# Vision tower on one core: attention weights turned three heads at a time and placed by nine transfers instead of six

## What is computed

```
h = patches @ W.T + b, class token in front, + pos_embed          # 64 x 37 x 256
q, k, v = h @ Wq, h @ Wkv                                         # 16 heads of 64
sim = q k^T * scale;  sim = sim + cope(q, sim, pos_emb)           # cope: gates, sum from the right, table lookups
attn = softmax(sim);  out = attn v;  h = layernorm(h + out @ Wout + b_out)
router = softmax(h @ router_w), top 2 of 8 experts, shared and routed feed-forward, layernorm
```

## Time and profile before

| | |
|---|---|
| median of 3 runs | 717.65 us (717.54 to 722.87) |
| the profiled execution's own time | 716.74 us |
| its span, first to last instruction | 715.0 us |
| TensorE busy, matmuls | 683.1 us, 96% of the span |
| VectorE busy | 489.1 us, 68% |
| ScalarE busy | 422.9 us, 59% |
| mean granted TensorE clock | 0.994 of full speed |

### The profile page before, as it was taken

How to read it: one execution, slowest core, us unless ns; L and a number is a source line. 1 busy time by engine, 2 the same in 40 slices (tenths; PEclk the granted TensorE clock), 3 DMA queues, 4 the chain that set the end, 5 groups by cost and what they waited for, 6 DMA issues and landing times.

```text
span 715.0 us, 14167 instructions
## 1 busy us (share of the span) xinstructions
PE 683.1 (96%) x4762; PEld 587.2 (82%) x4763; DVE 489.1 (68%) x1027; ACT 422.9 (59%) x730; POOL 123.0 (17%) x156
## 2 busy tenths in 40 slices
PE   8998999999999999999999999889999999999995
PEld 5897697978879696987969697658898999998884
DVE  3376787878978787897878789788962222332657
ACT  1563767576586657667675656544217777774453
POOL 2100000000000000000000000010014777775130
PEclk9999999999999999999999999999999999999998
DMA  9720321514132141414112103227304555552811
GB/s 274 224 66 16 77 60 35 95 47 103 49 80 74 36 94 48 99 54 94 43 41 58 47 18 104 85 88 237 128 15 108 146 138 131 145 130 57 286 69 54
DMA packets 81958, 67.16 MB, mean 94 GB/s; under 512 B 50646, under 2 KB 73196, under 8 KB 81928
## 3 DMA queue, kind: packets, MB, share of 16 engines
q1 hardware_dynamic: 76906, 56.30, 29.3%
q0 software_dynamic: 4224, 9.71, 4.5%
q10 hardware_dynamic: 798, 0.76, 0.3%
HBM read 35.60 MB, written 15.75 MB: 72 GB/s over the span
## 4 chain that ended last, share of the span: by engine, by line
PE 44%; DVE 34%; issue 9%; ACT 7%; DMA 4%; DVEq 1%; ACTq 0%; SPq 0%; POOLq 0%
PE ps_S L1419 11%; DVE table L1925 7%; PE ps_S L1150 7%; PE ps_S L1431 5%; PE ps_S L1352 3%; DVE u L1908 3%; DVE bit L1917 3%; PE ps_S L930 3%; PE ps_X L1025 2%; DVE nb L1937 2%; DVE nb L1940 2%; DVE mx L1947 2%; PE ps_X L1074 2%; DVE nb L1945 2%; PE ps_S L939 2%
## 5 line engine op out<-in xcount | busy, mean ns | idle before, releaser
L1419 PEld LDWEIGHTS ps_S<-attnT,v_sb 128*128 128x128 f32 x704 | 84.6, 192 | 4.6 <-ACT attnT L1772 2.1
L1419 PE MATMUL ps_S<-attnT,v_sb 128*128 128x128 f32 x704 | 85.8, 275 | 1.1 <-ACT attnT L1772 1.1
L1925 DVE COPY_PREDICATED table<-bit,table 111x112 f32<-111x112 int16 (+6 forms) x110 | 74.9, 681 | 11.2
L824 POOL TENSOR_TENSOR rs<-ve,neg_half 111x2 f32<-111x2 f32 x11 | 12.2, 1111 | 403.7 <-DVE ve L2011 403.7
L1025 PE MATMUL ps_X<-wkv_sb,hT 128*120 128x512 f32 (+1 forms) x176 | 81.3, 602 | 0.2 <-ACT v_sb L1529 0.2
L2356 DVE COPY attnT<-ps_S 128x256 f32<-128x256 f32 x44 | 18.7, 425 | 81.0 <-PE ps_S L1431 80.9
L1074 PE MATMUL ps_X<-oT,wout_sb 128*128 128x222 f32 x320 | 63.0, 354 | 0.0
L930 PE MATMUL ps_S<-hT,wq_sb 128*128 128x216 f32 (+1 forms) x320 | 61.6, 344 | 0.0
L1074 PEld LDWEIGHTS ps_X<-oT,wout_sb 128*128 128x128 f32 x320 | 59.3, 190 | 1.8 <-issue 1.8
L1025 PEld LDWEIGHTS ps_X<-wkv_sb,hT 128*120 128x120 f32 (+1 forms) x176 | 29.8, 181 | 35.0 <-issue 33.8
L930 PEld LDWEIGHTS ps_S<-hT,wq_sb 128*128 128x128 f32 x320 | 56.5, 188 | 1.3
(11 more groups left out here) (319 smaller groups left out, 1309.5 us busy)
## 6 DMA issues: line engine op xcount, KB each, us to landing
down_sb<-in_x_dram SPq DMA_DIRECT2D x10, 648.0 KB
attnT<-attn SPq DMA_DIRECT2D x117, 46.2 KB
gu_sb<-y_d SPq DMA_DIRECT2D x8, 512.0 KB, 6.6
h_d<-hT SPq DMA_DIRECT2D x11, 240.0 KB, 2.5
kept<-h_d SPq DMA_DIRECT2D x11, 240.0 KB, 2.8
h_d<-h SPq DMA_DIRECT2D x10, 222.0 KB
wkv_sb<-in_L_attn_Wkv_dram SPq DMA_DIRECT2D x2, 1024.0 KB, 12.2
gu_sb<-in_L_ffn_gate_w_dram SPq DMA_DIRECT2D x2, 1024.0 KB, 8.8
```

Source lines behind the costliest of these rows:

```text
L1419: mm = nc.tensor.matmul(S[:, i, j * FF + f * P:j * FF + f * P + P], held[:, i, k, j, f * P:f * P + P], xgT[:, i, k], start=(k == 0), stop= ...
L1925: A.did(V.copy_predicated(near[:, :, :, 0:SL - d], by_side(bit[:, n], r)[:, :, :, 0:SL - d], near[:, :, :, d:SL]))
```

## The change

Three heads are turned by one transpose, 120 columns; five such transposes and one of a single head (head 15) take the place of eight. They fill three places in each of the two banks instead of four. ScalarE's two copies have 120 partitions and 333 columns instead of 80 and 444. The placing has nine transfers, for three heads `j` and three images `b`; each carries six (`j = 0`) or five heads instead of eight, on 40 partitions as before. The slots of the heads in `attnT` are renumbered to fit. Which transfers ScalarE issues is now: none for even groups, the three of `j = 2` for odd groups, four for the last two placed groups. On TensorE the turn of the odd group moves behind `values(p, 1, 0)` in pairs 1 to 9. On ScalarE `gates` of the even group moves ahead of the second copy of values in pairs 2 to 10.

```diff
+        BLOCKS = -(-HEADS // TPG)
+        in_block = [len(range(j, HEADS, TPG)) for j in range(TPG)]
+        from_slot = [sum(in_block[:j]) for j in range(TPG)]
-        PLACES = 2 * TPG
+        PLACES = TPG * TPG
         def to_diagonal(j, b):
-            return (own_T[PAD * b:PAD * b + PAD, b, j * BLOCKS:j * BLOCKS + BLOCKS],
-                    turned_attn[PAD * j:PAD * j + PAD, b])
-        def in_two_queues(g):
-            return isinstance(g, int) and (g == 0 or g >= G - 3)
+            n, at = in_block[j], from_slot[j]
+            return own_T[PAD * b:PAD * b + PAD, b, at:at + n], turned_attn[PAD * j:PAD * j + PAD, b, :n]
+        def from_scalar(g, a):
+            if isinstance(g, int) and g >= G - 3:
+                return [(j, b) for j in (1, 2) for b in range(TPG)][:4]
+            return [(2, b) for b in range(TPG)] if a == 1 else []
...
-                for j in range(2 - in_two_queues(g)):
+                for j in range(TPG):
                     for b in range(TPG):
-                        sp.dma_start(*to_diagonal(j, b)).then_inc(placed[a], 16)
+                        if (j, b) not in from_scalar(g, a):
+                            sp.dma_start(*to_diagonal(j, b)).then_inc(placed[a], 16)
...
-                if ahead:
-                    turn_weights(p * 2 - 1, True)
-                    values(p, 1, 0)
-                else:
-                    values(p, 1, 0)
-                    turn_weights(p * 2 - 1, True)
+                values(p, 1, 0)
+                turn_weights(p * 2 - 1, True)
+                if not ahead:
                     for c in range(2):
                         turn(c)
                 values(p, 1, 1)
...
-                if in_two_queues(g):
-                    if g == 0:
-                        act.wait_ge(attnT_zeroed, 1)
-                    else:
-                        act.wait_ge(o_done, g * 2)
+                if from_scalar(g, a):
                     act.wait_ge(at_sb, g * 4 + 4)
-                    for b in range(TPG):
-                        act.dma_start(*to_diagonal(1, b)).then_inc(placed[a], 16)
+                    apart(act)
+                for j, b in from_scalar(g, a):
+                    act.dma_start(*to_diagonal(j, b)).then_inc(placed[a], 16)
...
+                if not next_first(p):
+                    gates(p, 0)
                 values(p, 0, 1)
                 if ahead:
                     weights(p * 2 - 1, 1)
                 if not next_first(p):
-                    gates(p, 0)
                     split(p - 2)
```

More of the change, by code:

```diff
@@ L149, in vit_tower @@
         own_attn = attn_flat[:, :HEADS * PAD].rearrange("p (h j) -> p h j", h=HEADS)
-        BLOCKS = HEADS // 2
-        PER_BANK = BLOCKS // 2
+        BLOCKS = -(-HEADS // TPG)
+        in_block = [len(range(j, HEADS, TPG)) for j in range(TPG)]
+        from_slot = [sum(in_block[:j]) for j in range(TPG)]
         turned_attn = (attn_flat[:, HEADS * PAD:HEADS * PAD + BLOCKS * TPG * TOK]
@@ L441, in heads_of @@
         def heads_of(n):
-            return slice(2 * n * PAD, 2 * n * PAD + 2 * PAD)
+            return slice(TPG * n * PAD, min(TPG * n + TPG, HEADS) * PAD)
         def to_diagonal(j, b):
-            return (own_T[PAD * b:PAD * b + PAD, b, j * BLOCKS:j * BLOCKS + BLOCKS],
-                    turned_attn[PAD * j:PAD * j + PAD, b])
-        def in_two_queues(g):
-            return isinstance(g, int) and (g == 0 or g >= G - 3)
+            n, at = in_block[j], from_slot[j]
[4 more added lines that the diff above has]
+            return [(2, b) for b in range(TPG)] if a == 1 else []
         def slot_of(h):
-            return h % 2 * BLOCKS + h // 2
+            return from_slot[h % TPG] + h // TPG
         def by_side(t, r):
@@ L1046, in turn_weights @@
                     heads_in = attn_flat[:r, heads_of(n)]
-                    mm = nc.tensor.transpose(S[:heads_in.shape[1], n // PER_BANK, n % PER_BANK * r:n % PER_BANK * r + r],
-                                             heads_in, ident[:r, :r])
-                    if n % PER_BANK == PER_BANK - 1:
+                    mm = nc.tensor.transpose(S[:heads_in.shape[1], n // 3, n % 3 * r:n % 3 * r + r], heads_in, ident[:r, :r])
+                    if n % 3 == 2:
                         mm.then_inc(at_done, 2)
@@ L1534, in weights @@
                     act.wait_ge(at_done, g * 4 + 2 * j + 2)
-                    nc.scalar.copy(turned_attn[:2 * PAD, :, PER_BANK * j:PER_BANK * j + PER_BANK],
-                                   S[:2 * PAD, j, :PER_BANK * ROWS].rearrange("p (n b q) -> p b n q", n=PER_BANK, b=TPG)
+                    nc.scalar.copy(turned_attn[:TPG * PAD, :, 3 * j:3 * j + 3],
+                                   S[:TPG * PAD, j, :3 * ROWS].rearrange("p (n b q) -> p b n q", n=3, b=TPG)
                                    ).then_inc(at_sb, 2)
-                if in_two_queues(g):
-                    if g == 0:
-                        act.wait_ge(attnT_zeroed, 1)
-                    else:
-                        act.wait_ge(o_done, g * 2)
+                if from_scalar(g, a):
                     act.wait_ge(at_sb, g * 4 + 4)
-                    for b in range(TPG):
-                        act.dma_start(*to_diagonal(1, b)).then_inc(placed[a], 16)
+                    apart(act)
+                for j, b in from_scalar(g, a):
+                    act.dma_start(*to_diagonal(j, b)).then_inc(placed[a], 16)
             def packed_weights(j):
```

## The result

The changed kernel takes **714.48 us** (median of 20 runs, 711.82 to 718.62) against 718.16 for the kernel before (20 runs, 716.95 to 722.87); ratio 0.9948, 95% interval 0.9930 to 0.9966. That is 0.5% faster where 1.0% was forecast (710.3 against 717.65), inside the range. The profiled execution took 714.02 (span 712.3) against 716.74 (715.0).

The account below looks back on a forecast made before the run. VectorE was taken to bound the loop, TensorE close behind and bounding after the change. Loop 7.45, start 0.2, pair 10 -0.3 sum to 7.35 us off 716.74: 709.4, median 0.9 above, so 710.3 us; range 705 to 715.5.

Parts of the forecast that it names:

- The loop: Pairs 2 to 9: period becomes 40.4 us, 0.9 less, with TensorE waiting 0.4 ahead of odd outputs; seven periods save.
- A: Rival, loop: a five-head transfer issues in 0.68 us or lands 0.4 sooner; period 40.0, total 707.4; chance 0.20.
- B: Rival, loop: transfers are slower by 0.5 us; period 40.9, total 713.8; chance 0.17.
- C: Rival, loop: issuers share one path, nine transfers take 6.8 us wherever issued; period about 42.6, total 728; chance 0.06.
- in the eighth, to pair 10, the queries are shorter and VectorE bounds alone, 1.15: Period from pair 9 to pair 10: with shorter queries VectorE alone sets it, saving 1.15 us.
- pair 10: I charge 0.3, bounds 0 and 1.5: Pair 10: SP issues five transfers, 1.5 us later, but loads queued ahead seem to set the landing; 0.3 us lost.
- TensorE's later wait of 1.7 absorbs group 20's delay: Group 20: ScalarE's fourth transfer delays the router's copies by 0.6 us, absorbed by TensorE's later 1.7 us wait for VectorE.
- a clock fall at the start: Pair 1: TensorE's clock falls to half in new idle time, so group 0's outputs take 1.7 us more.
- The start: Start: VectorE's wait for `distance` shrinks by 2.7 us; 0.2 of it is gained with a clock fall, 1.9 without.
- rival D: Start: no clock fall, all else as forecast, 1.7 us less; total 708.6; chance 0.12.

Follow-up runs that it names:

- e4: The changed kernel with SP issuing all nine odd transfers up to group 17: 743.38 us.
- full: The changed kernel itself, all parts of the change together: 714.48 us.
- e7: The kernel before with even gates between the value copies and the odd turn moved later, still two heads a turn and six transfers: 714.39 us.
- e6: The changed kernel, but outputs of group 19 wait for two copied chunks and only the scores behind them for all four: 713.38 us.
- e15: The changed kernel without the later odd turn (gates moved, three heads a turn, nine transfers): 708.23 us.
- e11: The changed kernel with ScalarE issuing three transfers instead of four in the last two placed groups: 713.24 us.
- e13_fill_sized: The changed kernel plus five matmuls nobody reads: two in pair 1, two ahead of group 19's outputs, one ahead of the router's transposes: 709.74 us.
- e8: The changed kernel with ScalarE issuing three of group 18's nine transfers and SP six: 716.23 us.
- e5: The kernel before with even gates between the value copies and all six of group 0's transfers issued by SP: 704.39 us.
- e14: e5 plus two matmuls nobody reads in pair 1: 703.81 us.
- e10: The changed kernel plus twelve matmuls nobody reads: five in pair 1, four ahead of group 19's outputs, three ahead of the router's transposes: 713.92 us.
- e12: e9 plus five matmuls nobody reads in pair 1: 705.78 us.
- e9: e5 with the edit of e6, group 19's outputs waiting for two copied chunks: 705.01 us.
- e1: The kernel before with only the even gates moved between the two value copies: 707.67 us.

## Why the prediction was wrong

**The loop was right.** Gates 1.4 earlier (1.3 forecast), odd placing landed 2.0 behind its last issue (284.07 to 286.06; 2.05 forecast), a wait of 0.50 (0.4 forecast), 40.37 (40.4). Rivals A and B fell by these rows, C by e4. One detail differs: the table copy at 313.32 shows no wait; VectorE waits 0.28 for the residual (296.40) instead, so TensorE's lateness enters there and not only by the scores. What I did not see is that of the three parts one makes the whole gain and one takes from it (the table above): the working went from the full change to one period and never asked for each part alone.

**The step "in the eighth, to pair 10, the queries are shorter and VectorE bounds alone, 1.15" failed**: +0.28 instead. VectorE does not bound alone: the table copy waits 1.30 for the score copies (435.38), so TensorE's lateness goes into it. Two things make TensorE late. One is the transfers: the shorter queries are the cover under which nine even transfers land. The forecast itself had only 0.5 left in the loop; with 1.5 us less of query products TensorE waits 0.94 (at 427.82). The other is the later turn. With both moves and six transfers (e7) the pair takes 40.93 and TensorE waits for no transfer, so nine cost 0.60; without the later turn it takes 40.12 with six and 40.82 with nine, so the turn costs 0.7 to 0.8.

**The step "pair 10: I charge 0.3, bounds 0 and 1.5" failed**, the largest miss: +3.66. It put two things at nothing: the clock, and the router's delay, which it took to be absorbed. The outputs of group 19 do start only 0.3 later behind T (+10.86, +10.55 before), but that figure was right by luck. It was charged for transfers held up by the loads, and what TensorE waits for in full is ScalarE's copies of the turned chunks, behind its four transfers (3.00 us at 439.93); when the outputs no longer wait for all four copies (e6), they start at +9.88. The new thing is that all of TensorE's idle time from the turn to these outputs now stands in one piece. Before it was three:

```profile
446.24 0.93 PE L1047 MATMUL ps_S<-ident,attn 111*80 111x111 f32 x8 [0.30 <-DVE attn L1975]
448.47 1.30 PE L1119 MATMUL ps_S<-ident,wkv_sb 128*128 128x128 f32 x8 [1.29 <-DMA wkv_sb<-h_d]
...
474.83 0.65 PE L1141 MATMUL ps_X<-ident,kT 8*128 8x8 f32 x8 [0.60 <-ACT qT L1578]
...
480.31 0.86 PE L1040 MATMUL ps_S<-ident,attn 101*37 101x101 f32 x8 [1.72 <-DVE attn L1963]
```

That is 0.30, 1.29 for a load and 1.25 for the transfers, 2.84 in all, against 2.98 in full. The load is no longer waited for there, because SP issues the loads at 432.18, 3.2 ahead of the late table copy, where it was 1.8 (441.52 and 443.33) before. Behind the one long idle time the clock fell, behind the three short ones it did not: outputs and scores take 5.45 instead of 3.85. That the fall came because the waits ran together is not tested by itself; e15, with 0.37 and 2.48, had no fall here. In the router's part the idle time grew from 0.60 to 1.66, 0.8 of delay by the fourth transfer (e11, with three, has 0.59), and the clock fell again: 1.5. Of this, the claim that TensorE's later wait of 1.7 absorbs group 20's delay was half right: it shrank to 1.08. Summed, 0.3 + 0.8 + 3.1 for the clock, less the 0.6 that the last wait gave up, is 3.6. The 3.1 is what e13_fill_sized wins in this stretch by removing the falls and no wait. I had charged a clock fall at the start, where TensorE idles, and had no term for one here.

**The start** came out 1.6 better, as rival D: no fall in pair 1 in this execution. But e6 and e8 show the fall there, at 2.7 rather than the 1.7 I charged. Forecast and rival each hold in some executions; the fall belongs into the spread, not into two cases.

**Behind the last product** the profiled execution lost 1.6 to no step of the change. The same code took 231.1 us in e11 and 233.5 in e8, where the clock fell once more at 539 us; in full it did not fall there. I put the 1.6 down to chance; its cause stays open.

Summed on the profiled executions: -7.35 forecast, +1.4 eighth period, +3.4 pair 10, -1.6 start, +1.6 behind the last product, -0.1 loop: -2.7, as measured. With the clock kept up the full change takes 709.7, and the forecast was 710.3. That closeness is partly luck: it hides the missed 1.4 behind the start's 1.6.

## What to carry to other kernels

Price each part of a change alone, and the last and first turns of a loop apart from its body: a cover that holds in the body (here 1.5 us of queries) may be missing there. When an engine takes over DMA issues, list what stands behind them on that engine in every stage, not in the loop only. Here an idle time of TensorE of 1.7 to 3 us cost, when the clock fell behind it, 1.2 to 2.7 us more (1.2 in e5 against e14, 2.67 in e6); look, too, whether waits that stood apart now run together. If the wait can't be removed, one or two matmuls that nobody reads, sized from a measured duration, took that cost away; too many gave it back (e10, e12).

## What the runs showed of the hardware

- The granted clock fell to 0.50 behind TensorE idle times of 1.66 and 2.98 us (full), 1.90 (e6) and 2.60 (e4); behind 1.25 us, 1.56 (e14, pair 10), 1.77 (e7, pair 10) and once behind 2.48 (e15, pair 10) it did not. Behind 2.46 us in pair 1 it fell in some executions (e5, e6, e8) and not in others of the same work (full, e9). Behind the 3.02 us of the earlier trace rows it fell before, and neither in e1 nor in e7. So the length of one idle time does not settle it. The Trainium skill (TensorE: Matmul & The Clock Gate, Part 1) says that the clock follows how busy TensorE has been recently, and that the point of the change varies from run to run; the runs agree.
- More work gave less time: with five matmuls added, 709.74 instead of 714.48 us, clock 0.996 to 0.998 against 0.982 to 0.994.
- Issuing one of these transfers takes 0.75 to 0.8 us on SP and 0.75 on ScalarE, side by side (six in 4.78, three in 2.25, at the same time), whether it has eight heads (six in 4.51 before) or five to six; where TensorE waited for it, the last landed 2.0 (full) to 2.1 us (e7) behind the start of its issue.
- A matmul of 128 x 512 f32 takes 0.91 us at full clock (two records of 0.46; five in 4.56 in e10).
